# All eight experts ordered by their token counts, with 1056 slots instead of 1144, the first expert's weights loaded by that order and in halves

## What is computed

```python
logits = xf @ Wg + bg                                  # 1024 tokens x 8 experts
one_hot = jax.nn.one_hot(jnp.argmax(logits, axis=-1), e, dtype=x.dtype)
h = jax.nn.gelu(jnp.einsum('td,edh->eth', xf, W1), approximate=True)   # D = 512, H = 2048
y = jnp.einsum('eth,ehd->etd', h, W2)
out = jnp.einsum('etd,te->td', y, one_hot)
```

## Time and profile before

| | |
|---|---|
| median of 3 runs | 782.52 us (781.96 to 782.92) |
| time of the profiled execution | 782.04 us |
| span of the profiled execution | 780.2 us |
| mean granted TensorE clock | 0.988 |
| PE busy | 756.3 us, 97% |
| DVE busy | 579.5 us, 74% |
| ACT busy | 474.8 us, 61% |
| POOL busy | 249.7 us, 32% |

### The profile page before, as it was taken

How to read it: one execution, slowest core, us unless ns; L and a number is a source line. 1 busy time by engine, 2 the same in 40 slices (tenths; PEclk the granted TensorE clock), 3 DMA queues, 4 the chain that set the end, 5 groups by cost and what they waited for, 6 DMA issues and landing times.

```text
span 780.2 us, 21321 instructions
## 1 busy us (share of the span) xinstructions
PE 756.3 (97%) x8460; PEld 442.6 (57%) x8460; DVE 579.5 (74%) x1077; ACT 474.8 (61%) x850; POOL 249.7 (32%) x407
## 2 busy tenths in 40 slices
PE   9899999999999999999999999998799999999996
PEld 3455545555455554555445745456587687677773
DVE  4986767677676876666665677798899968879982
ACT  5556676557665666655755315323686686798871
POOL 0145244432454224442243110002134334144440
PEclk9999999999999999999999999999699999999998
DMA  8324453344233441445331711111599999899920
GB/s 306 155 66 113 122 148 91 91 111 111 41 86 96 111 110 36 113 100 138 57 100 34 194 75 54 60 50 38 177 344 397 410 381 353 325 342 382 400 75 30
DMA packets 94855, 125.30 MB, mean 161 GB/s; under 512 B 76369, under 2 KB 79185, under 8 KB 83909
## 3 DMA queue, kind: packets, MB, share of 16 engines
q1 hardware_dynamic: 92404, 117.67, 46.8%
q0 software_dynamic: 2384, 6.75, 2.4%
HBM read 100.22 MB, written 6.75 MB: 137 GB/s over the span
## 4 chain that ended last, share of the span: by engine, by line
PE 87%; DVE 6%; ACT 2%; issue 1%; DMA 1%; POOL 1%; SPq 1%; POOLq 0%; DVEq 0%; ACTq 0%
PE bank L1592 66%; PE bank L1987 9%; PE bank L1761 4%; PE bank L1727 3%; PE bank L1958 2%; DVE arena L990 2%; ACT arena L707 1%; DMA arena<-in_wv_t 1%; DVE arena L1027 1%; PE bank L1605 1%; DVE arena L1005 1%; PE bank L1916 1%; PE bank L1945 1%; POOL arena L504 0%; PE bank L1896 0%
## 5 line engine op out<-in xcount | busy, mean ns | idle before, releaser
L1592 PE MATMUL bank<-arena 128*128 128x512 f16 (+12 forms) x3880 | 543.7, 300 | 5.5 <-DVE arena L1429 1.0
L1592 PEld LDWEIGHTS bank<-arena 128*128 128x128 f16 (+3 forms) x3880 | 305.7, 99 | 232.2 <-issue 9.1
L707 ACT ACTIVATE arena<-arena 128x256 f16<-128x256 f32 (+8 forms) x302 | 251.9, 883 | 19.7 <-PE bank L1958 6.0
L990 DVE SCALAR_TENSOR_TENSOR arena<-arena 128x2048 f16<-128x2048 f32 (+4 forms) x101 | 200.4, 2005 | 29.7 <-ACT arena L707 28.1
L707 ACT ACTIVATE arena<-bank 128x512 f16<-128x512 f32 (+1 forms) x110 | 63.2, 591 | 102.1 <-PE bank L1592 69.8
L990 DVE SCALAR_TENSOR_TENSOR arena<-bank,arena 128x512 f16<-128x512 f32 (+1 forms) x109 | 73.2, 684 | 53.2 <-ACT arena L707 52.1
L1987 PE MATMUL bank<-arena 128*128 128x512 f16 x384 | 86.2, 379 | 0.0
L566 POOL TENSOR_TENSOR arena<-arena 32x1024 f16<-32x1024 f32 (+1 forms) x16 | 35.2, 2200 | 150.8 <-PE bank L1761 150.6
L714 ACT ACTIVATE arena<-bank,arena 128x512 f16<-128x512 f32 (+1 forms) x68 | 44.6, 665 | 57.7 <-PE bank L1592 55.8
L1017 DVE SCALAR_TENSOR_TENSOR arena<-bank,arena 128x512 f16<-128x512 f32 x64 | 47.5, 748 | 41.3 <-ACT arena L714 41.3
L745 ACT ACTIVATE arena<-arena 128x257 f32<-128x257 f32 x128 | 63.1, 498 | 0.0
(11 more groups left out here) (133 smaller groups left out, 520.8 us busy)
## 6 DMA issues: line engine op xcount, KB each, us to landing
arena<-in_w SPq DMA_DIRECT2D x64, 1024.0 KB, 5.9
arena<-in_ctx_t SPq DMA_DIRECT2D x15, 1024.0 KB, 5.3
arena<-in_awt SPq DMA_DIRECT2D x3, 1024.0 KB, 7.1
l_dram<-arena SPq DMA_DIRECT2D x4, 512.0 KB, 4.3
x_dram<-arena SPq DMA_DIRECT2D x1, 2048.0 KB, 12.8
arena<-in_wk_t SPq DMA_DIRECT2D x4, 256.0 KB, 4.5
arena<-in_ctx_t SPq DMA_DIRECT2D x4, 256.0 KB, 5.8
arena<-in_wv_t SPq DMA_DIRECT2D x1, 1024.0 KB, 8.7
```

What stands on the lines that cost most here:

```text
L707: return a.activation(dst, src, ACT.Copy, scale=scale)
L990: return v.scalar_tensor_tensor(dst, src, scale, h, ALU.mult, ALU.subtract)
L1592: last = m.matmul(out_ap, w, x, start=(n == 0), stop=(n == len(pairs) - 1))
```

## The change

Six things change.

- The places get 160, 160, 144, 136, 120, 136, 112 and 88 slots (1056 in all; before 1144). All eight are filled by the order of the counts, through `RANK_AT`. With the counts above, they hold 160, 158, 143, 132, 116, 131, 106 and 78 tokens, so no further round follows. Before, the places held 78, 143, 160, 158, 132, 106, 131 and 116 tokens in 160, 160, 160, 160, 136, 112, 136 and 120 slots. Places with two parts are five instead of six.
- The early loads and splits of the first expert's pieces are gone. SP loads them once `expert_order` has signalled `ordered`. The first two pieces are loaded, and split by ACT and DVE, in two halves each, so that step 0 of H needs half a piece only.
- `expert_order` stands ahead of the first gather on DVE, and the count matmuls ahead of the rank matmuls on PE.
- The first expert's rank is picked out by the order (`first_rank`): one multiplication and one reduction more.
- In the first expert all six remaining pieces are split between the steps of H and after them, and those of the next expert later than before. `sort_ids` is done in step 4, on all eight places.
- POOL's first gather waits for `ids_sorted`, where it waited for `ids_done`. The store of x2 is issued earlier on SP.

```diff
-CAPS = (160, 160, 160, 160, 136, 112, 136, 120)
-STATIC = 2
-RANK_AT = (0, 1, 2, 3, 4, 7, 5, 6)
+CAPS = (160, 160, 144, 136, 120, 136, 112, 88)
+HALVED = 2
+RANK_AT = (0, 1, 2, 3, 5, 4, 6, 7)
...
-            for k in range(PIECES - 1):
-                sp.wait_ge(s["e_lo"], from_zero(k - 3))
-                load_piece(0, 0, k)
...
+            sp.wait_ge(s["ordered"], 1)
+            first = sp.value_load(order[0:1, 0:1], min_val=0, max_val=E - 1)
+            for k in range(HALVED):
+                load_halves(first, k)
+            for k in range(HALVED, PIECES):
+                if k == 6:
+                    sp.wait_ge(s["l2_stored"], 64)
+                    sp.wait_ge(s["xs_done"], 2)
+                load_piece(first, k)
+            with sp.Fori(1, E) as e:
+                expert_pieces(e, e)
...
-                if n in EARLY_PIECES:
-                    piece_hi(0, EARLY_PIECES.index(n))
...
-            for k in range(4, PIECES - 2):
-                piece_hi(0, k)
+            for k in range(HALVED):
+                halves_hi(k)
...
+                    if first:
+                        if k % 2 == 0:
+                            piece_hi(0, HALVED + k // 2)
...
+            def own_slots():
+                dve.wait_ge(s["rank_ps"], 1)
+                chained(v.scalar_tensor_tensor(slot_of, BD[:, 0:NT * E].rearrange("p (t e) -> p t e", e=E), 1.0, onehot16,
+                                               ALU.add, ALU.mult))
+                chained(v.tensor_tensor(score, slot_of, by_tile(place[:, 0]), ALU.mult))
+                chained(v.reduce_max(first_rank, score, AX_X))
+                slots(first_rank)
...
                 if first:
-                    slots(slot_of[:, :, 0])
-                    dve.wait_ge(s["count_ps"], 1)
-                    v.tensor_copy(counts, BE[:, 0:E]).then_inc(s["chain_dve"], 1)
-                    dve.wait_ge(s["chain_dve"], next(chain))
-                    piece_lo(0, 4)
+                    expert_order()
+                    own_slots()
                     for c in range(KC):
                         first_gathered(c)
+                    for k in range(HALVED):
+                        halves_lo(k)
                     slots(own_rank)
-                    piece_lo(0, 5)
```

More of the change, by code:

```diff
@@ L155, in perceiver_block @@
         own_ids = keep.take([NT, E, 2], F16)
-        own_rank = keep.take([NT], F32)
+        own_rank, first_rank = (keep.take([NT], F32) for _ in range(2))
         id_offset = keep.take([2], F32)
@@ L680, in round_ @@
             def round_(r, first=False):
[L681 to L684 removed]
+                pool.wait_ge(s["ids_sorted"], r * 9 + 9)
                 pool.sem_inc(s["pool_waits"], 1)
@@ L963, in experts @@
             def experts(r):
-                expert(r * E, prev=False)
+                expert(r * E, prev=False, first=is_first(r))
                 if is_first(r):
@@ L1900, in _ @@
             pe.wait_ge(s["onehot_done"], 1)
+            product(BE[:, 0:E], [(ones16, onehot16[:, k, :]) for k in range(NT)]).then_inc(s["count_ps"], 1)
             m.matmul(BD[:, 0:NT * E], tri16, onehot16.rearrange("p t e -> p (t e)"), start=True, stop=False)
@@ L1906, in _ @@
             last.then_inc(s["rank_ps"], 1)
-            product(BE[:, 0:E], [(ones16, onehot16[:, k, :]) for k in range(NT)]).then_inc(s["count_ps"], 1)
             def first_gather():
```

152 lines of the change are left out of this document (72 added, 80 removed).

## The result

The changed kernel takes 788.95 us (median of 5 runs, 787.58 to 790.42), the kernel before 782.92 us beside it (781.96 to 784.75): ratio 1.008, 95% interval 1.0068 to 1.0092. That is 0.8% slower, and above the forecast range of 779.2 to 786.3.

The account below looks back on a forecast made before the run. PE, almost without a gap in the expert phase, was taken as the bound. Span 780.2 + 9.9 (first expert) - 10.0 (later experts) = 780.1, as a median 782.4, plus 0.2 for semaphores: 782.6 us, range 779.2 to 786.3.

Parts of the forecast that it names:

- the long wait: First expert's H, behind step 1: PE waits 2.2 us for DVE's `slots(own_rank)`, which comes after the fourth half piece, until 574.5.
- the term for the halves' landing: First expert's loads: half pieces land 1.5 us apart, at 566.2, 567.7, 569.2 and 570.7.
- rival 2: Slower by the clock: new PE waits in the first expert drop it, 1.7 us per fall, total 784.3 to 786.0; chance 0.26.
- the gathered tokens: First expert's end: tokens land 11.9 us after the sorted list, at 597.1, so PE waits 2.5 us before the transposes.
- So no further wait: Second expert: DVE has the pieces done before PE needs them and loads keep pace, so PE waits no more.
- 10.0 us less: Seven later experts, second H to last Y's end: 168.3 us against 178.3 before, from fewer slots.
- The cost of the order: First expert: late, ordered loads and their waits start the second expert at 604.8 instead of 594.94, 9.9 us later.
- The gain: Seven later experts: narrower places, one fewer with two parts, save 10.0 us.
- no change: Whole kernel: loss and gain cancel to no measurable change, 782.6 us, between 781.0 and 784.1; chance 0.39.
- Rival 3: Slower by the first expert: DVE late with each late load, second expert starts after 606.5, total 785; chance 0.09.
- Rival 4: Faster: gather lands as PE gets there, no random waits, ACT not holding place 4 or 7; 779.5 us; chance 0.26.

Follow-up runs that it names:

- experiment 1: Changed kernel with the old slots and the old order of places by rank, leaving only the late, ordered loads: 793.41 us, ratio 1.0160 to before.
- one_input: Changed kernel plus two DVE maximum reductions over perm, one input in SBUF, in the second expert: 781.88 us, ratio 1.0018 to before.
- two_inputs: Changed kernel plus two DVE instructions with two inputs in SBUF, at the same places as in one_input: 787.11 us, ratio 1.0095 to before.
- after_third: Changed kernel unaltered, run again on chip 13: 784.61 us, ratio 1.0061 to before.
- perm_early: Changed kernel with slots(own_rank) on DVE between the first two half pieces instead of behind the fourth, chip 0: 780.43 us, ratio 0.9995 to before.
- fillers: Changed kernel with ten unused matmuls of 512 columns on PE ahead of the token numbers, chip 0: 782.24 us, ratio 1.0022 to before.
- perm_again: Same kernel as perm_early, changed kernel with slots(own_rank) between the first half pieces, on chip 13: 780.14 us, ratio 1.0013 to before.
- experiment 7: Kernel before, changed kernel, and its variants with filler matmuls and with early slots(own_rank), one run each, chip 0: 781.53, 790.80, 785.69 and 783.68 us.
- shifted: Changed kernel with ten small matmuls of 8 columns on PE ahead of the first gather, chip 1: 789.3 us, ratio 1.0090 to before.
- before_b: Kernel before, unaltered, run once more on chip 0 in the set of experiment 7: 781.53 us.
- perm_b: Changed kernel with slots(own_rank) between the first two half pieces, one run on chip 0 in the set of experiment 7: 783.68 us.

## Why the prediction was wrong

**The first expert, as forecast until the long wait.** H starts at 568.78 (forecast 568.95). The wait for `slots(own_rank)` is 2.59 us (2.2); it ends at 575.9 and not 574.5, since the second half of the first piece landed 3.2 us after the first and not 1.5 (ACT's first two halves start at 565.89 and 569.11). The order, the first load at 561.87 (562.4) and the hidden table load were right. So the term for the halves' landing was 1.4 us too early.

**Then the clock, rival 2.** It fell in all four traces of the changed kernel, between 575 and 577 us, for 6.8 us in the first and 3.4 us in the others. The forecast weighed this at 0.26 and left it out of the sum, and argued against it with the full matmuls before and behind the wait; that argument was wrong. Its price, put at 1.7 us a fall, was 1.2 (3.4 us at half) and 2.6 (6.8 us) in the matmuls of H. H ended at 589.7, not 585.5: 1.4 from the late start, the rest clock and small waits. The sort then ended at 588.60 (585.2), but the gathered tokens landed 10.8 us behind it (11.9), so of 4.2 us in H 2.2 were left: second H at 607.0, forecast 604.8. The Trainium skill, TensorE: Matmul & The Clock Gate, section on HAM oscillation, says that waits for data between short bursts put the array back to half rate. The trace agrees, here with a wait of 2.59 us behind bursts of 1.8 us.

**The step that failed most: "So no further wait" and "10.0 us less".** The sum was 168.3 us of later places; the trace has 174.6. The slots' own price of 10.0 came near: 9.6 us in experiment 1 and 8.7 on chip 13, both with the long scatter. By place (forecast, then measured): 28.0, 27.6; 26.6, 29.7; 25.6, 26.3; 22.1, 23.3; 25.6, 26.3; 21.7, 22.9; 18.7, 18.4. So 3.1 of the 6.3 us are in place 2 and 3.8 in places 3 to 6, less 0.7 at the ends.

Place 2: the forecast itself had DVE busy without a gap until 610.4 and asked only whether the pieces are in time. What it missed is POOL: the scatter's issue is held behind DVE's chain of instructions with two inputs in SBUF, the rows of x2 come 9 us late, DVE (in order) stands still for them, and its low halves and pieces are late for PE. one_input and two_inputs show this chain of effects. In the changed kernel it costs 1.7 us where nothing else disturbs (after_third and perm_early, 28.01 and 28.09, against 26.33 in fillers, perm_again and one_input). In the first trace itself PE has no wait for DVE in place 2: the 3.4 us above 26.33 are stops of PE (0.32, 0.95, 0.46 and 0.48 us stand in the timeline above) and longer runs of matmuls around them. With stops and a long scatter place 2 lasts 28.9 to 30.0, with stops and a short one 26.8 to 27.4, so the scatter weighs there too; how is not shown. Before, the same kinds of instruction stood on DVE and the scatter took 2.8 us. It ended at 602.79, 0.1 us into DVE's gap of 0.49 us, too early for the gap to have released it, so why it was not held isn't known.

Places 3 to 6, and the rest of place 2: PE stops without a releaser, as in the stops of 0.32 and 0.95 us before 641.39 and 642.83 in PE's timeline of the changed kernel. They stand in the traces of the first pair, of chip 1 and, in part, of the set of experiment 7, not in the first set on chip 0 nor on chips 12 and 13 (there at most one in place 4, which lengthens nothing), where these places last 25.29, 22.13, 25.29 and 21.62 us. In places 4 and 6 they work through the other engines too: ACT waits 1.09 and 1.20 us for PE's bank at 696 and 746 us, where it waits for nothing on chip 13, DVE's pieces come later, and PE waits 1.23 and 1.56 us for DVE ahead of the next H, against 0.33 and 1.20. That is 0.9 and 0.4 of the 1.2 and 1.3 us that these two places are longer. In places 3 to 6 they are independent of the scatter (shifted has a short one and 26.28, 23.36, 26.27, 22.93). The kernel before showed them much less in the same sets (before_b: 25.57, 21.83 and 25.63 in its places of 136, 112 and 136 slots, against 25.29, 21.82 and 25.29 on chip 13). That the supply of PE's instructions is slower where a place has fewer columns and so more instructions per us is only argued, and perm_b speaks against it as the whole cause. So 3.8 of the 6.3 us, and at least a part of the 3.1 in place 2, have a cause that stays open.

**The balance.** The cost of the order was forecast at 9.9 and was 12.1 us in the first pair, 11.0 on chip 13 and 12.9 in the set of experiment 7. The gain was forecast at 10.0 and was 3.7 in the first pair, 8.7 on chip 13 (177.1 to 168.4) and 3.6 in that set. With the long wait taken out and, in its trace, the scatter short (perm_again) the kernel stands at 1.0013 (0.9998 to 1.0028): the "no change" of the forecast, but of a kernel with one more edit. Rival 3 (DVE late by the landings, second H after 606.5) came true in its place in the first trace, and by its cause in part: the late landing gave 1.4 us, the clock 2.6. Rival 4 had nothing, since the gather still ended last.

## What to carry to other kernels

An estimate that says "this engine is busy without a gap from here to there" is not at its end when the work itself is in time: ask which other engine needs that gap. Price a half-clock stretch into the sum where the change adds such a wait between short bursts of matmuls; here, with waits of 2.6 to 2.8 us, it cost 1.2 to 2.6 us of matmul time. Set variants against each other in one set of runs, since the same kernel's later places differed by 6 us between sets (168.4 and 174.9). And where experts of fixed places cost little to load early, narrowing their places (0.46% here, if the counts allow it) came cheaper than ordering them (11 to 13 us of exposed chain); joining the early `slots(own_rank)` with a one-input instruction in DVE's long stretch wasn't tried.

## What the runs showed of the hardware that was not expected

- The issue of an indirect DMA by POOL lasted 3.14 us or 19.35 us by the kind of the instruction added on DVE, a reduction or one of two inputs in SBUF, of 1.48 us both; it ended 0.97 to 0.99 us after the start of the first instruction that had not two inputs in SBUF. The Trainium skill, SBUF — State Buffer, section on who interferes with whom, says that a DVE instruction with two inputs in SBUF contends with a GpSimd instruction that reads SBUF. The long scatters agree; that a chain of such instructions can hold POOL for its whole length is what they add. The issues of 2.75 and 1.00 us among such instructions show that it doesn't always.
- The clock fell about a wait of 1.50 us in shifted and of 3.39 us in two_inputs, and did not in perm_again, with waits of 0.74 and 1.49 us in that stretch. In perm_early and fillers it fell behind H instead, about 588.5 and 590.4 us, for 3.4 us each. So it isn't the length of a single wait that decides.
- Unexplained stops of PE of 0.2 to 1 us, and the waits behind them, made the same four places 4.5 us longer in some sets than in others (26.27, 23.34, 26.30, 22.93 against 25.29, 22.13, 25.29, 21.62).
